# A perceiver block on one core: TensorE's attention loop ordered by two tiles, and 16-bit keys written straight from PSUM

## The reference, cut

```python
def rmsnorm(t): return t * rsqrt(mean(t * t, -1) + 1e-6)
# cross attention of 64 queries on 6272 context rows, 32 heads of 8
q = layernorm(x) @ Wq.T                       # 64 x 256
kv = context @ [Wk; Wv].T                     # 6272 x 512, split per head into k and v
attn = softmax(rmsnorm(q) . rmsnorm(k) * 8 ** -0.5)
x = x + attn @ v
# then self attention (16 heads of 128, weights = 4-bit codes times block scales)
x = x + mxfp4_attention(layernorm(x))
# then a shared and 8 routed experts, top 2
x = x + experts(layernorm(x))
```

## Time and profile before

| | |
|---|---|
| median of 3 runs | 217.31 us (215.54 to 218.15) |
| the profiled execution | 218.6 us, span 216.8 us |
| TensorE busy (matmul) | 203.2 us, 94% of the span |
| ScalarE | 148.8 us, 69% |
| VectorE | 133.0 us, 61% |
| GpSimd | 108.3 us, 50% |
| chain that ended last | 81% on TensorE: values 20%, projection 32%, scores 11% |
| means, ScalarE | exponential 1.03 us, square 0.38, logarithm 0.33, k_r 0.23 |
| means, VectorE | context high part 0.29, sum of squares 0.42, values out 0.41, key product 0.42, 16-bit key copy 0.80 |
| means, GpSimd | context low part 0.74, third key part 0.67, dequantisation 2.38 |
| turned keys, from issue to landing | 3.8 us |

### The profile page before, as it was taken

One profiled execution on the slowest core, in us unless ns is written; L12 is line 12 of the kernel. 1 busy time (PEld: TensorE's weight loads), 2 busy tenths in 40 slices (PEclk: granted clock), 3 DMA queues, 4 the chain that ended last, 5 costly groups with the idle time before them and its releaser, 6 DMA issues.

```text
span 216.8 us, 7144 instructions
## 1 busy us (share of the span) xinstructions
PE 203.2 (94%) x2625; PEld 131.9 (61%) x2625; DVE 133.0 (61%) x339; ACT 148.8 (69%) x289; POOL 108.3 (50%) x127
## 2 busy tenths in 40 slices
PE   7787999999999999999999999999977899989695
PEld 4355666666666666667667666766645535485364
DVE  1788867757576675857677575866740453625730
ACT  2557798887988888888889888888997233402520
POOL 5346777758576575867657576765833000000000
PEclk9999999999999999999999999999999999999957
DMA  6689999999999897989979795999748990000000
GB/s 202 190 191 217 179 210 267 175 236 166 237 252 183 234 194 202 230 168 254 189 211 208 211 279 182 260 209 219 184 97 187 412 436 26 0 3 3 0 0 12
DMA packets 66546, 39.65 MB, mean 183 GB/s; under 512 B 53858, under 2 KB 60642, under 8 KB 66402
## 3 DMA queue, kind: packets, MB, share of 16 engines
q1 hardware_dynamic: 66098, 38.98, 76.5%
q10 hardware_dynamic: 432, 0.46, 0.6%
HBM read 26.52 MB, written 0.07 MB: 123 GB/s over the span
## 4 chain that ended last, share of the span: by engine, by line
PE 81%; DVE 7%; ACT 4%; issue 4%; DMA 2%; POOL 1%; DVEq 0%; ACTq 0%; POOLq 0%
PE ps L849 20%; PE ps L869 13%; PE ps L827 11%; PE ps L872 10%; PE ps L875 9%; PE ps L914 5%; PE ps L1024 3%; PE ps L784 3%; DMA kT<-k 2%; ACT room L444 2%; PE ps L966 2%; PE ps L923 1%; PE ps L953 1%; PE ps L1016 1%; POOL k L371 1%
## 5 line engine op out<-in xcount | busy, mean ns | idle before, releaser
L444 ACT ACTIVATE room<-ps 128x1024 f32<-128x1024 f32 x98 | 100.3, 1029 | 19.1 <-PE ps L827 19.1
L384 POOL TENSOR_TENSOR ctx_lo<-ctx_f,ctx_hi 128x256 fp32r<-128x256 f32 x49 | 36.5, 745 | 48.1 <-DVE ctx_hi L607 45.1
L849 PE MATMUL ps<-room,v_sb 128*27 128x192 f32 (+1 forms) x1176 | 52.6, 312 | 0.4 <-ACT room L444 0.4
L869 PE MATMUL ps<-wkv_hi,ctx_hi 128*128 128x512 f32 x98 | 43.7, 446 | 0.9 <-DVE ctx_hi L607 0.5
L639 DVE CAST k<-k_n 128x512 f16<-128x512 f32 x49 | 39.2, 801 | 2.6
L872 PE MATMUL ps<-wkv_lo,ctx_hi 128*128 128x512 f32 x98 | 39.0, 398 | 0.9 <-DVE wkv_lo L560 0.9
L849 PEld LDWEIGHTS ps<-room,v_sb 128*27 128x27 f32 (+1 forms) x1176 | 31.2, 103 | 13.4 <-ACT room L444 0.9
L366 POOL TENSOR_TENSOR w_all<-w_all,s_ring 128x1024 f32<-128x1024 f32 x16 | 38.0, 2376 | 0.0
L371 POOL TENSOR_TENSOR k<-k_n,k 128x256 f16<-128x256 f32 x49 | 33.0, 674 | 7.1 <-DVE k L639 7.1
L631 DVE TENSOR_TENSOR k_n<-ps,k_r 128x256 f32<-128x256 f32 x49 | 20.8, 424 | 24.3 <-ACT k_r L472 24.3
L827 PEld LDWEIGHTS ps<-q_blk,kT 48*128 48x128 f16 x784 | 22.1, 94 | 21.8 <-issue 13.2
(11 more groups left out here) (119 smaller groups left out, 132.0 us busy)
## 6 DMA issues: line engine op xcount, KB each, us to landing
w_all<-codes SPq DMA_DIRECT2D x16, 512.0 KB, 3.9
ctx_f<-ctx_t SPq DMA_DIRECT2D x48, 128.0 KB, 2.7
up_sb<-up_w SPq DMA_DIRECT2D x5, 704.0 KB, 7.3
s_ring<-scales SPq DMA_DIRECT2D x12, 256.0 KB
s_ring<-wo_scales SPq DMA_DIRECT2D x4, 512.0 KB
dn_sb<-down_w SPq DMA_DIRECT2D x1, 1792.0 KB, 13.1
kT<-k SPq DMA_TRANSPOSE x49, 3.8
wkv_f<-xwkv SPq DMA_DIRECT2D x1, 256.0 KB, 3.9
```

Of the source, the lines that this page charges most:

```text
L384: nc.gpsimd.tensor_tensor(ctx_lo[:, split.slot(2)], ctx_f[:, split.slot(4)], ctx_hi[:, split.slot(2)].bitcast(F32), ALU.subtract).then_inc ...
L444: nc.scalar.activation(probs[:, t.slot(2), half], ps_scores[half].rearrange("p b n -> p (b n)"), ACT.Exp).then_inc(exp_done, 1)
L849: last = nc.tensor.matmul(ps_o[group // 2][CT * j:CT * j + heads * VW, at:at + heads * N], v_sb[:, t.slot(8), slot:slot + heads].rearrange ...
L869: nc.tensor.matmul(dst, ctx_hi[:, a, c], wkv_hi[:, c], start=(c == 0), stop=False)
```

## The change

TensorE: steps are now paired. An odd step does its scores and two projections (c + 5 and c + 6), the even step behind it its scores and two value steps (c - 2 and c - 1). `probs` has three slots. ScalarE: in an odd step both exponentials and then the square of c + 5; in an even step the square of c + 5, the logarithm and `k_r` of c + 4, both exponentials, the logarithm and `k_r` of c + 5. In step 0: both exponentials of tile 0, then square, logarithm, `k_r` of tile 4 and then of tile 5. VectorE: the second key operation no longer copies `k_n` but multiplies the PSUM keys by `k_r` once more, straight into the two 16-bit parts, without the wait between the two; only this second one signals `kn_done`, for which TensorE, GpSimd and ScalarE wait. VectorE and GpSimd keep their order of work. `KV` and `TR` are one more, the written-out prologue runs to step 3, the hardware loop from 4 to 35.

```diff
-PROJ, KV, TR, PV = 5, 4, 3, -1
-FIRST, LAST = -(PROJ + 1), T - PV
-HEAD = KV
-LOOP0 = 1 - PV
-ITERS = (T - PROJ - 1 - LOOP0) // U
+PROJ, KV, TR, PV = 5, 5, 4, -1
+FIRST, LAST = -(PROJ + 2), T - PV
+HEAD = 4
+LOOP0 = 4
+ITERS = (T - PROJ - 2 - LOOP0) // U
...
+    def odd(self):
+        return self.c % 2 == 1
+
+    def probs_slot(self):
+        return 0 if self.odd() else 1 + self.c // 2 % 2
...
@@ GpSimd
-                wait(pool, k1_done, keys.count(plus=1))
+                wait(pool, kn_done, keys.count(plus=1))
...
-                u, piece = divmod(c - DEQ0, DEQ)
+                u, piece = divmod(c + 1 - DEQ0, DEQ)
...
@@ ScalarE
             def step(t):
+                r = t.ahead(KV)
+                if t.i is None and t.c <= 0:
+                    if t.c == 0:
+                        exps(t, 0)
+                        exps(t, 1)
+                    for k in ((r.ahead(-1), r) if t.c == 0 else (r,)):
+                        if k.exists() and t.c != -1:
+                            keys_squared(k)
+                            keys_rms(k)
+                elif t.odd():
+                    for half in range(2):
+                        if t.exists():
+                            exps(t, half)
+                    if r.exists():
+                        keys_squared(r)
+                else:
+                    if r.exists():
+                        keys_squared(r)
+                    if r.ahead(-1).exists():
+                        keys_rms(r.ahead(-1))
+                    for half in range(2):
+                        if t.exists():
+                            exps(t, half)
+                    if r.exists():
+                        keys_rms(r)
...
@@ VectorE, keys_scaled
-                    k_r[:, r.slot(2)].unsqueeze(2).to_broadcast([P, XH, XD]), ALU.mult).then_inc(kn_done, 1)
-                wait(dve, kn_done, r.count(plus=1))
+                    k_r[:, r.slot(2)].unsqueeze(2).to_broadcast([P, XH, XD]), ALU.mult)
...
-                pairs = k_n[:, r.slot(2)].rearrange("p (r h d) -> p r h d", h=2, d=XD)
-                nc.vector.tensor_copy(key_parts(r)[:, :, :, 0:2, :], pairs.unsqueeze(3).to_broadcast(
-                    [P, PAIRS, 2, 2, XD])).then_inc(k1_done, 1)
+                nc.vector.tensor_tensor(
+                    key_parts(r)[:, :, :, 0:2, :],
+                    kv_bank(r)[:, 0:D].rearrange("p (r h d) -> p r h d", h=2, d=XD).unsqueeze(3).to_broadcast([P, PAIRS, 2, 2, XD]),
+                    k_r[:, r.slot(2)].rearrange("p (r h) -> p r h", h=2).unsqueeze(3).unsqueeze(4).to_broadcast([P, PAIRS, 2, 2, XD]),
+                    ALU.mult).then_inc(kn_done, 1)
...
@@ TensorE
             def step(t):
...
+                elif t.odd():
+                    for k in (kv, kv.ahead(1)):
+                        if k.exists():
+                            project_context(k)
+                else:
+                    for pv in (t.ahead(PV - 1), t.ahead(PV)):
+                        for group in range(len(GROUPS)):
+                            if pv.exists():
+                                values(pv, group)
```

More of the change, by code:

```diff
@@ L377, in _ @@
                 t = Tile(None, c)
-                split, keys = t.ahead(PROJ + 1), t.ahead(TR)
-                if keys.exists() and c < 0:
+                split, keys = t.ahead(PROJ + 2), t.ahead(TR)
+                if keys.exists() and c < -1:
                     second_part(keys)
@@ L442, in exps, with keys_squared @@
                 wait(act, scores_mm, t.count(2, half + 1))
-                wait(act, pv_done, t.count(2, half - 3))
-                nc.scalar.activation(probs[:, t.slot(2), half], ps_scores[half].rearrange("p b n -> p (b n)"),
+                wait(act, pv_done, t.count(2, half - 3 if t.odd() else half - 7))
+                nc.scalar.activation(probs[:, t.probs_slot(), half], ps_scores[half].rearrange("p b n -> p (b n)"),
                                      ACT.Exp).then_inc(exp_done, 1)
[L447 to L456, removed]
+            def keys_squared(r):
+                wait(act, kv_mm, r.count(plus=1))
+                wait(act, ss_done, r.count(plus=-1))
+                nc.scalar.activation(k_sq[:, r.slot(2)], kv_bank(r)[:, 0:D], ACT.Square).then_inc(sq_done, 1)
@@ L457, in step @@
                 if r.i is None and r.c == 1:
                     queries_rms()
-                if r.i is None and 0 <= r.c < HEAD:
+                if r.i is None and r.c < HEAD:
                     nc.scalar.activation(v_sb[:, r.slot(8), :, 0:XD], kv_bank(r)[:, D:2 * D].rearrange(
                         "p (h d) -> p h d", d=XD), ACT.Copy).then_inc(v_done, 1)
[L463 to L470, removed]
-                    wait(act, kn_done, r.count(plus=-1))
-                    nc.scalar.activation(k_r[:, a], k_ln[:, a], ACT.Exp, scale=-0.5).then_inc(r_done, 1)
@@ L474, in _, with keys_rms @@
-            steps(act, step, {-4: queries_copied})
+            def keys_rms(r):
+                a = r.slot(2)
+                wait(act, ss_done, r.count(plus=1))
+                nc.scalar.activation(k_ln[:, a], k_ss[:, a], ACT.Ln, bias=eps_rms[:],
+                                     scale=1.0 / XD).then_inc(ln_done, 1)
+                wait(act, ln_done, r.count(plus=1))
+                wait(act, kn_done, r.count(plus=-1))
+                nc.scalar.activation(k_r[:, a], k_ln[:, a], ACT.Exp, scale=-0.5).then_inc(r_done, 1)
@@ L476, in _ @@
+            steps(act, step, {-5: queries_copied})
             act.wait_ge(pv_done, 2 * T)
@@ L618, in values_copied @@
                 wait(dve, kv_mm, r.count(plus=1))
-                wait(dve, pv_done, r.count(2, -10))
+                wait(dve, pv_done, r.count(2, -14))
                 if r.i is None and r.c == HEAD:
@@ L882, in step @@
                         scores(t, half)
-                for group in range(len(GROUPS)):
-                    if pv.exists():
-                        values(pv, group)
-                if t.i is None and t.c == 0:
-                    project_context(kv.ahead(-1))
-                if kv.exists() and not (t.i is None and t.c == -1):
-                    project_context(kv)
+                if t.i is None and t.c <= 0:
+                    if t.c == 0:
+                        project_context(kv.ahead(-1))
+                    if kv.exists() and t.c != -1:
+                        project_context(kv)
+                elif t.odd():
[7 more added lines that the diff above has]
+                                values(pv, group)
             steps(pe, step, {-5: queries_mm, -2: queries_turned})
```

17 lines of the change are left out of this document (9 added, 8 removed).

## The result

| | median of the executions | span of the profiled one |
|---|---|---|
| before | 217.73 us (4, 215.54 to 220.03) | 216.8 |
| changed | 223.66 us (4, 222.41 to 225.5) | 221.6 |

A forecast was written before the change was run, and what follows sets the result against it. TensorE bounds the kernel, 6.31 us a pair; ScalarE would hold the new order at 6.20. Reaching the last context projection 4.1 late and a tail 0.4 longer, 4.6 before rounding, added to 217.3 give 221.9 us; range 215.5 to 227.

The forecast's parts named there:

- second key operation: VectorE's new multiplication of 512 elements out of PSUM takes 0.69 us, bounds 0.43 and 0.85, and GpSimd does not hold it.
- projection 8; loss at the start: Start: TensorE waits for keys of tiles 4 and 5, so this projection starts at 31.6, not 28.6: 3.0 us lost.
- undisturbed pair: Loop pair without dequantisation interfering: period 6.20 us set by ScalarE, against 6.31 before; TensorE waits 0.19 a pair.
- TensorE alone, a pair: Loop: TensorE's own work for two tiles, 0.55 + 3.00 + 0.55 + 1.91 = 6.01 us, 0.30 less than before.
- held context copy, six pairs: Odd steps 5, 11, ... 35: GpSimd's dequantisation holds VectorE's context copy, making P2 0.50 late: 3.0 us in all.
- dequantisation on even steps: Loop, even steps: GpSimd's dequantisation costs nothing, at most 0.1; counted as 0.05 for seven, 0.35 us.
- projection 48: End of the loop: starts at 31.6 + 20 x 6.20 + 3.0 + 0.35 = 158.9, against 154.82 before, 4.1 late.
- The circle: Loop: from second projection's results through ScalarE's square, logarithm, k_r and two exponentials to the next pair; no quicker than 6.20 us.
- The tail: From the last context projection to the last values: 15.7 us against 15.3, two value steps standing ahead of tile 47's scores; 0.4 more.
- The clock: Rival at the start: TensorE's waits lower its granted clock for 6.8 us, 3.4 lost, 225.3 us in all; chance 0.22.
- The other side, TensorE staying the bound: Rival in the loop: ScalarE's chain shorter, context copies not held, pairs 6.01, 6.0 saved, 214.7 us; chance 0.17.
- third rival: Loop: product costs 0.85, giving 226 us, or joins save nothing, pair 6.31, giving 223.7 us; chance 0.08.

The follow-up runs named there:

- rms_and_context: Changed kernel with logarithm and k_r of a pair's first tile in the odd step, and the loop's second context copy ahead of the first tile's key products: 213.43 us, 0.983.
- rms_early: Changed kernel with ScalarE's logarithm and k_r of a pair's first tile moved into the odd step, behind its square: 222.28 us, ratio 1.031 to the kernel before.
- pairs_old_keys: Changed kernel with the old VectorE part (product, wait, 16-bit copy, kn_done with the first product): 224.77 us.
- tail_alone: Changed kernel with values one tile at a time from step 45 on, after the last projection: 219.39 us, ratio 1.019 to the kernel before.

## Why the prediction was right, and where its terms were off

| step | forecast | measured |
|---|---|---|
| projection 6, waiting for keys 4 | 23.94 | 24.07 |
| projection 7, waiting for keys 5 | 26.80 | 27.00 |
| projection 8; loss at the start | 31.6; 3.0 us | 31.86; 3.2 us, 3.0 from projection 5 on |
| undisturbed pair | 6.20 | 6.16 to 6.21 |
| TensorE alone, a pair | 6.01 | 5.98 (rms_and_context) |
| second key operation | 0.69, not held | 0.68, not held |
| held context copy, six pairs | 6 x 0.50 = 3.0 us | 2.5 us |
| dequantisation on even steps | 0.35 us | nothing seen |
| return of the hardware loop | not counted | 4 x 0.20 = 0.8 us |
| projection 48 | 158.9 | 158.89 |
| from there to the last values | 15.7 | 16.1 (14.6 to 14.7 where the clock kept up) |
| whole | +4.6 us | +4.9 us in the profiled executions, +5.9 in the medians |

*What bounds it.* Right: TensorE was saturated before, and ScalarE was next. The circle gave 6.20, and rms_early shows that it is the circle: take 0.5 out of it and the pair is TensorE's.

*VectorE and the keys.* Right, and the product had the size of the row of L683. Counted from the pair's start at 95.53 the dequantisation began at 3.40 (3.43 forecast), the copy ended at 5.93 (5.95), the logarithm came at 6.29 (6.31), the product ended at 7.93 (7.96), the late projection started at 8.08 (8.12). The term was too large by 0.5 us in all, since one of the six pairs lost 0.28 only and the others a little under 0.50; the 0.35 for even steps should have been left out. The product was right in size; its later release at the start, which the forecast has in its 3.0 us, is worth 0.2 there by pairs_old_keys.

*The missing term.* 0.8 us, at the places of the loop's return. In the kernel before all pairs but one take 6.29 to 6.31, so it is not seen there, nor in rms_and_context. The loop's total came out right to 0.3 us (127.35 against 127.03) because this cancels with three terms that were too large: the 3.0, the 0.35, and the circle, by up to 0.04 a pair. That agreement is luck, and so is that of projection 48 to 0.01: it began 0.3 late and the loop was 0.3 short.

*The tail.* The mechanism was right, two value steps stand before the scores of tile 47. The size was off both ways: up to there the exponentials ran 0.7 earlier than counted, as the exponentials of tile 43 began with projection 48 (158.88) and its square stood 1.8 and not 2.4 behind that. At a full clock the tail would have been 0.5 us shorter than before (14.7 against 15.2 from the same place), where 0.4 longer was forecast. Then the clock fell, which the prediction had only placed at the start, and cost 1.4. So the tail's 16.1 beside 15.7 is luck, and with it part of the agreement of the whole, 4.9 beside 4.6: without the fall the profiled execution would have lost 3.6.

*The rivals.* The clock was a rival of its own with 0.22 at the start. It does fall there in some executions (rms_early, where it cost 2.0 and not the 3.4 counted, and tail_alone, 0.2) and in the tail in others. The median lies 1.8 above the forecast, and part of that may be the clock: the changed kernel's four executions had mean grants of 0.969 to 0.977, the profiled one of the kernel before 0.984. The other side, TensorE staying the bound, was right about its condition: where ScalarE's circle is shorter and the copy not held, a pair is 5.98 and the kernel faster than before. The changed kernel did not meet it. That the new product is dearer than counted, or that the joins save nothing (third rival), is excluded: the product took 0.68, its loop is as long with the old keys, and the joins saved 0.33 a pair in rms_and_context. At the start the product's later release costs some 0.2, as above.

## What to carry to other kernels

When an order saves the saturated engine something, add up the circle that runs through the next engine, from release to release, before counting the saving; here 0.12 of 0.33 us a pair was left, and moving two small operations into that engine's idle time gave the rest. A pairing lengthens every first dependence, so it costs at the start and at the end, where nothing lies between a result and its use; there single steps are better. And an operation that is off the critical path in the old order (a copy that GpSimd holds up) must be placed anew against its neighbour's timetable, not just costed.

## What the hardware showed

- A release crosses engines in 0.04 us from projection to square (98.58 to 98.62), 0.05 from exponential to scores (101.33 to 101.38), and from square to sum in 0.03 in fifteen and 0.12 in three of the eighteen cases in which VectorE stood idle for it in the changed kernel. Where the hardware loop begins or returns, ScalarE's chain took some 0.2 longer (1.06 and not 0.87 from scores to exponential), which was not expected; that the loop is the cause is argued.
- A VectorE copy of 256 elements between SBUF tiles, met by a GpSimd multiplication, ends 0.15 after it; such copies took up to 1.27 us in the changed kernel and 1.75 in rms_early, against 0.29. When one such copy is taken away, the next takes over the wait.
- The granted clock fell from 1.00 (2.4 GHz) to 0.50 (1.2 GHz) behind stretches in which TensorE was busy 1.30 of 3.35 and 1.54 of 3.00 us, the second with no single wait above 0.6. It stayed down for 6.83 and 3.41 us. Stretches as idle left it at 1.00 in other executions (1.26 of 3.35 and 1.53 of 3.00 us, both above). I had looked for it only where one wait was long.
- Joining two projections saved TensorE 0.20 us (in rms_and_context 3.00 from the first one's start to the scores behind the second, where two single ones took 2 x 1.60), joining two value steps 0.13 (1.87 against 2 x 1.00). By an estimate from these two, 0.07 to 0.10 us goes into each change from one kind of matmul to another.
